# Shared expert at the head of each slot, and the second half's routing moved into the slots, in a two-layer attention and mixture-of-experts kernel

## The reference, cut to what matters

```
xn = layernorm(x)
x  = x + attention(xn) + ffn(xn)

attention: q, k, v = linear(xn); for each row position the 8 batches attend to
           each other in 16 heads of 8 features; then an output product and bias
ffn:       scores  = sigmoid(xn @ w_gate.T)                  # 16 experts
           allowed = the 2 of 4 groups with the highest sum of their two best scores
           chosen  = the 4 best allowed experts; w = their scores / (their sum + 1e-6)
           routed  = sum over experts of w[e] * (silu(xn @ w1[e].T) * (xn @ w3[e].T)) @ w2[e].T
           shared  = (silu(xn @ w1s.T) * (xn @ w3s.T)) @ w2s.T        # no weight
           ffn     = routed + shared
```

## Time and profile before

| what | value |
|---|---|
| median of 3 executions | 382.11 us (381.07 to 382.5) |
| the profiled execution's own time | 381.5 us |
| its span, first to last instruction | 379.7 us |
| mean granted TensorE clock | 0.968 |
| stage one, until the last chunk's `xT_lo` is done | about 170 us |
| stage two, from PE's first gate product to the last DVE instruction | 174.2 to 377.0 us |
| busy in the span: DVE, PE, POOL, ACT | 317.0, 311.3, 244.4, 188.2 us |

### The profile page before, as it was taken

The page is one execution under the profiler, slowest core; times in us unless marked ns, Lnnn a source line. Parts: engine busy times, 40 slices in busy tenths (PEclk is TensorE's granted clock), DMA queues, the critical chain, the costliest instruction groups (busy, mean ns, idle before and its releaser), DMA issues.

```text
span 379.7 us, 5029 instructions
## 1 busy us (share of the span) xinstructions
PE 311.3 (82%) x1435; PEld 226.0 (60%) x1435; DVE 317.0 (83%) x831; ACT 188.2 (50%) x505; POOL 244.4 (64%) x162
## 2 busy tenths in 40 slices
PE   0177777798988987776598898899999999899894
PEld 0045665696776966665365565575766666576562
DVE  3874899969787576974899999989898998989792
ACT  0553756768687668546153253352635253352621
POOL 9144758737356371005388876889998898987661
PEclk9996999999999999869699999999999999999999
DMA  7740000000000000001871331543535343334001
GB/s 189 239 136 0 1 2 1 3 1 0 3 0 3 0 2 1 0 2 54 166 182 56 94 89 58 137 102 97 105 81 135 92 106 90 96 102 135 1 24 31
DMA packets 20367, 24.81 MB, mean 65 GB/s; under 512 B 2140, under 2 KB 11028, under 8 KB 20340
## 3 DMA queue, kind: packets, MB, share of 16 engines
q1 hardware_dynamic: 18544, 23.53, 23.9%
q0 software_dynamic: 544, 0.43, 0.7%
q10 hardware_dynamic: 1252, 0.53, 0.5%
HBM read 22.13 MB, written 2.36 MB: 64 GB/s over the span
## 4 chain that ended last, share of the span: by engine, by line
DVE 35%; PE 35%; issue 11%; ACT 9%; POOL 4%; DMA 3%; ACTq 1%; SPq 1%; DVEq 0%; POOLq 0%
PE Q L871 15%; PE VK L871 7%; PE T L871 5%; DVE att L1495 4%; PE ND L871 4%; DVE hid L1532 4%; DVE sgc L1519 3%; POOL prod_qk L811 3%; DVE rope_a L1274 3%; DVE rope_b L1276 3%; PE T L867 2%; DVE attn L1306 1%; DMA headmask<-in_c_headsel 1%; ACT L707 1%; ACT xn L565 1%
## 5 line engine op out<-in xcount | busy, mean ns | idle before, releaser
L811 POOL TENSOR_TENSOR prod_qk<-qkv 128x1024 f32<-128x1024 f32 x32 | 76.2, 2396 | 21.1 <-ACT qkv L526 12.2
L821 POOL TENSOR_TENSOR prod_pv<-prob,qkv 128x1024 f32<-128x1024 f32 x32 | 69.6, 2195 | 16.5 <-DVE att L1495 15.0
L871 PE MATMUL VK<-hid,w 128*128 128x512 f32 x144 | 74.6, 599 | 0.9 <-DVE hid L1532 0.9
L707 ACT ACTIVATE ND<-Q 128x512 f32<-128x512 f32 x64 | 37.2, 582 | 74.8 <-PE Q L871 58.7
L871 PE MATMUL Q<-xT_hi,w_hi 128*128 128x512 f32 x72 | 52.1, 723 | 1.2 <-issue 0.7
L1519 DVE TENSOR_TENSOR sgc<-ND,cw 128x512 f32<-128x512 f32 x64 | 43.6, 681 | 6.5 <-ACT ND L707 5.0
L1532 DVE TENSOR_TENSOR hid<-T,sgc 128x512 f32<-128x512 f32 x64 | 43.4, 678 | 0.3 <-issue 0.2
L871 PE MATMUL Q<-bias,ones 128*128 128x400 f32 (+1 forms) x64 | 29.9, 467 | 16.7 <-DVE xT_lo L1325 9.1
L1481 DVE TENSOR_REDUCE scr<-prod_qk 128x128 f32<-128x1024 f32 x32 | 38.8, 1212 | 4.5 <-POOL prod_qk L811 4.4
L871 PE MATMUL T<-xT_hi,w_hi 128*128 128x512 f32 x72 | 30.5, 423 | 13.0 <-DVE hid L1532 13.0
L1495 DVE TENSOR_REDUCE att<-prod_pv 128x128 f32<-128x1024 f32 x32 | 38.2, 1195 | 0.0
(11 more groups left out here) (184 smaller groups left out, 755.2 us busy)
## 6 DMA issues: line engine op xcount, KB each, us to landing
cw<-comb_table SPq DMA_DIRECT2D x64, 256.0 KB, 4.6
out_x<-fin SPq DMA_DIRECT2D x8, 256.0 KB, 4.4
x<-in_x SPq DMA_DIRECT2D x2, 256.0 KB, 4.6
wraw<-in_w1T SPq DMA_DIRECT2D x1, 512.0 KB, 10.3
w3raw<-in_w3T SPq DMA_DIRECT2D x1, 512.0 KB, 5.7
w<-in_w2T SPq DMA_DIRECT2D x1, 512.0 KB, 6.4
rope_c<-in_c_cos SPq DMA_DIRECT2D x1, 256.0 KB, 5.0
rope_s<-in_c_sin ACTq DMA_DIRECT2D x1, 256.0 KB, 5.6
```

The costliest lines, as they stand in the source:

```text
L707: act.activation(gated[:, :], QB[side(n, s)][:, :], ACT.Silu).then_inc(sg_ready, 1)
L811: pool.tensor_tensor(prod_qk[:, t % 2], bc(qkv2[:, TH * half + t, j, 0:D], 1, NB), qkv2[:, :, j, D:2 * D], ALU.mult).then_inc(qk_prod, 1)
L821: pool.tensor_tensor(prod_pv[:, t % 2].rearrange("p (h e) b -> p b h e", e=HD), bc(prob[:, t].rearrange("p h b -> p b h"), 3, HD), qkv2[:, ...
L871: return pe.matmul(o, lhsT, rhs, start=start, stop=stop)
```

## The change

Four edits. The shared slice becomes s = 0 and the routed ones s = 1 to 8, so the first slice of stage two needs no weights from the table. The transposes of the first half's weights, and ACT's evacuation of them, move ahead of the last chunk's four `l1_tile`s. PE starts stage two when all but the last of these tiles are evacuated, and waits for the last before slice 1. On ACT, `sigmoid(1)` moves from ahead of the loop to slice 6, behind that slice's Silu and ahead of the first exponential; on DVE the second half's routing, whose first three parts stood ahead of the loop and whose others stood at slices 0 to 16, moves to slices 8 to 22; the second transposes of weights move from slice 20 to 28 (`COMB_AT`), and PE's first wait for them from unit 1 to unit 2.

```diff
-        COMB_AT = BASE[0] + 15
+        COMB_AT = BASE[1] + 14
+        def routed_slice(s):
+            return s - 1
...
-                l1_tile(0)(NB - 1)
-                l1_tile(1)(NB - 1)
                 combT_evac(0)
-                l1_tile(2)(NB - 1)
-                l1_tile(3)(NB - 1)
+                for j in range(NJ):
+                    l1_tile(j)(NB - 1)
...
-            sigmoid(1)
             exp_done = exp_of(act)
             def gate(n, s):
                 act.wait_ge(g_ps, NS * n + s + 1)
-                if s >= 2:
-                    act.wait_ge(sgc_ready, (NS - 1) * n + s - 1)
+                if s >= 3:
+                    act.wait_ge(sgc_ready, (NS - 1) * n + s - 2)
                 else:
                     after(act, hid_ready, NS * n + s - 1)
-                gated = SB[side(n, s)] if s < NS - 1 else sg
+                gated = SB[side(n, s)] if s > 0 else sg
...
                     if p == 1:
+                        if u == 0:
+                            sigmoid(1)
                         exp_done(u)
...
+                if at(i, STEPS - 1):
+                    comb_transposes(0)
                 run(i, 4, l1_tile(0))
                 run(i, 2, output_product)
                 run(i, 4, l1_tile(1))
-                if at(i, STEPS - 1):
-                    comb_transposes(0)
...
-            pe.wait_ge(l1_kept, NT)
+            pe.wait_ge(l1_kept, NT - 1)
...
-                w = slice(s * P, (s + 1) * P)
+                at = routed_slice(s) % NS
+                w = slice(at * P, (at + 1) * P)
+                if n == 0 and s == 1:
+                    pe.wait_ge(l1_kept, NT)
...
-                        if u == 1:
+                        if u == 2:
                             pe.wait_ge(combT_ready, 2)
...
                 if k == COMB_AT:
-                    pe.wait_ge(fin_ready, 1)
+                    pe.wait_ge(fin_ready, 2)
...
             def weighted(n, s, k):
-                if s < NS - 1:
+                if s > 0:
+                    r = routed_slice(s)
                     dve.wait_ge(sg_ready, NS * n + s + 1)
-                    if s % 2 == 0:
-                        dve.wait_ge(ld_cw[s // 2], 32 * (n + 1))
+                    if r % 2 == 0:
+                        dve.wait_ge(ld_cw[r // 2], 32 * (n + 1))
...
             def route_second(k):
-                if k == 0:
+                if k == 8:
+                    route_pairs(1)
+                if k == 9:
+                    route_groups(1)
+                if k == 10:
+                    route_above(1)
+                if k == 11:
                     route_limits(1)
-                if k == 1:
+                if k == 12:
                     route_masked(1)
-                if k == 5:
+                if k == 13:
                     route_top(1)
-                if k in (9, 11):
-                    route_chosen(1, (9, 11).index(k))
-                if k == 13:
+                if k in (15, 17):
+                    route_chosen(1, (15, 17).index(k))
+                if k == 19:
                     route_weights(1)
-                if k == 14:
+                if k == 20:
                     route_sums(1)
-                if k == 15:
+                if k == 21:
                     route_parts(1)
-                if k == 16:
+                if k == 22:
                     route_comb(1)
...
-            route_pairs(1)
-            route_groups(1)
-            route_above(1)
             for k in range(LAST):
```

More of the change, by code:

```diff
@@ L1044, in down @@
                     after(pe, yT_ready, n)
-                mm(VK[:, :], w2[:, s, :], hid[:, s % 3, :], s == 0, s == NS - 1).then_inc(y_ps, 1)
+                mm(VK[:, :], w2[:, routed_slice(s) % NS, :], hid[:, s % 3, :], s == 0, s == NS - 1).then_inc(y_ps, 1)
             def down_two_before(n, s):
@@ L1513, in weighted @@
             def weighted(n, s, k):
-                if s < NS - 1:
+                if s > 0:
+                    r = routed_slice(s)
                     dve.wait_ge(sg_ready, NS * n + s + 1)
-                    if s % 2 == 0:
-                        dve.wait_ge(ld_cw[s // 2], 32 * (n + 1))
-                    V.tensor_tensor(sgc[:, k, :], SB[k][:, :], cw[:, s // 2, s % 2, :], ALU.mult)\
+                    if r % 2 == 0:
+                        dve.wait_ge(ld_cw[r // 2], 32 * (n + 1))
+                    V.tensor_tensor(sgc[:, k, :], SB[k][:, :], cw[:, r // 2, r % 2, :], ALU.mult)\
                         .then_inc(sgc_ready, 1)
             def hidden(n, s, k):
-                if s < NS - 1:
-                    dve.wait_ge(sgc_ready, (NS - 1) * n + s + 1)
+                if s > 0:
+                    dve.wait_ge(sgc_ready, (NS - 1) * n + s)
                 else:
@@ L1530, in hidden @@
                 after(dve, y_ps, NS * n + s - 2)
-                src = sgc[:, k, :] if s < NS - 1 else sg[:, :]
+                src = sgc[:, k, :] if s > 0 else sg[:, :]
                 V.tensor_tensor(hid[:, s % 3, :], UB[k][:, :], src, ALU.mult)\
```

## The result

The changed kernel takes 387.58 us (median of 4 executions, 386.19 to 387.97), the kernel before 381.59 (4, 380.64 to 382.5) beside it: ratio 1.0135, interval 1.0109 to 1.0161. It is slower by 1.35%, 6.0 us. The profiled execution took 387.23, its span is 385.4.

The account below looks back on a forecast made before the run. DVE was taken to set the pace while the second half's routing runs. -4.2 + 4.5 - 0.3 + 0.6 + 3.4 = +4.0 us gave 385.5 from the profiled 381.5, or 386.1 on the median's scale; range 381.0 to 390.0.

Parts of the forecast that it names:

- Steps 1 and 2: Start of stage two: weights leave 2.68 us earlier, first `sgc` at 179.5; shared slice's `hid` (0.60) done in DVE's wait.
- Steps 3 and 4: Slices 1 to 7: DVE ready at 192.95, but Sigmoid in ACT's list puts `sgc` 7 at 195.6: -4.2 us.
- Step 5: Second half's routing in slices 8 to 22 costs DVE +4.5 us at unblocked lengths; filled idle time gives -0.3.
- The `sgc` that DVE owes: By `sgc` 7 DVE has done one `sgc` fewer than before; it shows in the last slice: +0.6 us.
- Step 6: Routing instructions blocked by POOL's products: pairs +2.1, above +1.2, limits and masked +0.1, together +3.4 us (0 to 7.2).
- counted as unchanged: Routing parts in slices 19 to 22, weights to `comb`, were partly blocked before too: no change in cost.
- rival B: Later slots close up with the shared slice first, at most 1.0 us per slot, six over six slots; chance 0.16.
- A: Rival: the moved routing isn't blocked by POOL, so the sum is +0.6 and the time 382.7 us; chance 0.27.
- C: Rival: exponential needs no table load behind Sigmoid; `sgc` 7 comes 1.3 us earlier, 384.8; within the forecast's 0.57.
- The edits at nothing: Later second weight transposes and the gate's wait for `hid` cost nothing; the two trips end by slice 33, needed at 37.

Follow-up runs that it names:

- the kernel with the group scores in PSUM: Changed kernel with the second half's group scores reduced a second time into a PSUM bank, which above reads as one input; 384.84 us, ratio 1.0065.
- POOL held twice: Changed kernel with POOL's third value product of unit 0 held until pairs are done and its next score product until above is done; 383.07 us, ratio 1.0027.
- POOL held once: Changed kernel with POOL's next score product in unit 0 held until above is done; 387.54 us, ratio 1.013.
- the version that beats both: Changed kernel with sigmoid and routing, also limits and masked, ahead of the loop, and POOL's second score product held until masked is done; 378.12 us, ratio 0.9889.
- the first weights early alone: Kernel before, with only the first weights' transposes and their evacuation moved ahead of the last four tiles; 380.44 us, ratio 0.9957.
- late again: Changed kernel with the first weights' transposes and their evacuation put back between the last tiles; 392.21 us, ratio 1.0268.
- the version with the shared slice last: The version that beats both, but with the shared slice last in each slot again; 378.22 us, ratio 0.9894.

## Why the prediction was right, step by step

The sign and the forecast were right, and no rival came true. The sum was +4.0, and the two traces differ by 5.7; the terms are compared with the trace of after. Their errors cancel in part: two are 0.4 too high, two came out 1.85 and 0.75 too low.

**Steps 1 and 2 held.** The transposes stand at 168.94, the first `sgc` starts at 179.40 (179.5), the shared slice's `hid` ends at 176.76 (176.5).

**Steps 3 and 4 held.** `sgc` 7 starts at 195.25 with 2.37 of wait for ACT in front (195.6 and 2.65): -4.6 for -4.2. From Silu 6 to `sgc` 7 it takes 6.19, for 6.15. PE didn't come back slowly: its first up pass took 0.49 after 2.54 of waiting. That it didn't was luck in part: with the same code, in the kernel with the group scores in PSUM, it did after 2.41, and `sgc` 7 came 0.8 later. (For that case the prediction added 1.65, where its rows give 4.06 - 2.25 = 1.81; the range hardly changes by it.)

**Step 5** was 0.4 too high. Counted from the start of each piece to the start of what follows it, and unblocked, the routing takes 4.1 in the slots and not 4.5: pairs 0.64 and above 0.63 (with POOL held twice), groups 0.46, limits 0.57 (1.27 less the 0.7 below), masked 0.33, top 1.44. The first half's rows hold pauses between the pieces that the slots don't have. With the blocked terms below it adds up: 4.1 - 0.3 + 6.65 - 1.4 = 9.05 from `sgc` 7 to `sgc` 23, and the windows give 53.04 - 44.03 = 9.01. The `sgc` that DVE owes, 0.6, stands.

**Step 6 is the one that was mis-sized.** Pairs: 2.21 less the 0.26 of the third one alone, +1.95 for +2.1; it was the third instruction that was caught, not the second. Above: +1.2 was taken from bounds of 0 and 4.4, nearer to 0, "because no row shows instructions this small beside POOL". From the first of above to `hid` it is 212.07 - 207.42 = 4.65, and 206.41 - 205.78 = 0.63 with POOL held: **+4.0**. Size is no cover: an instruction of 16 elements waited for a whole product. And the reason was wrong as it stood, for the trace of before has such a row:

```profile
223.21 0.95 DVE L1416 TENSOR_SCALAR wsum<-wsum 128x16 f32<-128x16 f32 x1
```

It took 0.18 in the first half and ends here at 224.16, with a POOL product that ran from 221.76 to 224.14. Here the rule of the Trainium skill (SBUF — State Buffer, SBUF: two separate sides) was the better guide, and the sentence that gave its term, nearer to 4.4, has the right number; the kernel with the group scores in PSUM agrees with its condition too, since one input outside SBUF was enough to pass at 0.17 to 0.20. Limits: 0.92 less 0.20, +0.7 for +0.1.

**What "counted as unchanged" gave back.** Weights to `comb` met POOL less often than before: `comb` 0.41 for 1.43, and the other two 0.38 less in sum: -1.4.

So step 6 was +6.65 - 1.4 = +5.25 in place of +3.4. The last piece, +0.75, is what the shared slice first costs at slices 44 and 53: the version with it first and the one with it last show it with no routing in it. It was named, as what speaks against rival B, and wasn't in the sum. -4.6 + 9.0 + 0.6 + 0.75 = +5.75; the last `fin` is 5.73 later.

**The rivals.** A needed short instructions beside a busy POOL: the trace shows blocked ones, and taking most of the blocking away gives 383.07, close to A's 382.7. The closeness is luck: in that kernel the limit is still blocked for 2 us, and without that the terms as measured give about -0.85 (-4.6 + 4.1 - 0.3 - 1.4 + 0.6 + 0.75) where A had +0.6. B needed later slots below 22.8; they take 23.8 and 23.3 as before. C needed the exponential to do without a load: there is one at 191.40. The trace agrees with the Trainium skill (ScalarE: Activation LUTs, Table sets: the hidden batching unit) in that Sigmoid and Exp have different sets.

**The edits at nothing.** DVE's idle time in front of `sgc` that ended with `cw` is 2.64 in sum, all at the first: no later transfer was late. The groups of the page of after show it:

```profile
L1526 DVE TENSOR_TENSOR sgc<-ND,cw 128x512 f32<-128x512 f32 x64 | 43.5, 680 | 9.7 <-ACT ND L708 7.0
```

9.7 of idle time, 7.0 of it ended by ACT.

**Where the gain went.** The first weights were really early, worth 1.5 alone. But DVE's wait for them had been the place for the routing, free of charge; moved into slices that DVE paces, its pieces cost their full length, and met POOL besides.

**What stays open.** Why three of four executions with POOL held once showed none of the 2.4 us that the fourth gained. And why PE's clock falls after a wait in one execution and not in another.

## What to carry to other kernels

Before work is moved out of a wait, look for what the engine does in its new place: an idle stretch that looks like a stall may be where work is done for nothing. An instruction's price is the one it has beside its neighbours there: a small VectorE instruction with both inputs in SBUF can cost as much as the GpSimd instruction that runs beside it, so hold GpSimd for the microsecond that the small ones need, or put one input in PSUM. And when one start comes earlier, move into the shorter wait what still fits: here pairs to masked, 3.8 us, and the time fell by 1.1%.

## What the runs showed of the hardware

- Of DVE's small instructions beside a busy POOL, `TENSOR_TENSOR` with both inputs in SBUF waited (0.18 became 2.37), with one in PSUM it didn't (0.17). The limit, a `TENSOR_SCALAR` with one SBUF input, was blocked as well: 0.92, 2.25 and 2.26 where it takes 0.20 alone. A `TENSOR_REDUCE` wasn't: rank took 0.40 and 0.41 beside the products in the two kernels with POOL held, and 0.42 in the first half, alone.
- POOL gets in between two DVE instructions that follow each other without idle time: at 209.36 its second product and the second of above were both due, and POOL went first.
- PE's wait alone doesn't tell whether its clock falls. It kept 2.4 GHz after waits of 1.65 us (the version that beats both) and 2.54 (the changed kernel), and came back at 1.2 GHz after 4.19 (the first weights early alone) and 4.91 (late again), for 5.4 and 5.8 us. Between these it went either way: after 2.41 in the kernel with the group scores in PSUM and 2.51 in the version with the shared slice last, the granted clock was 0.73 over the 6 us that follow. Nor does what PE did just in front of the wait. The two traces of the changed kernel have the same wait, 2.08 us up to 198.31 and 198.49, with PE busy for 6.07 and 6.05 of the 6.20 us in front; over the next 6 us the granted clock was 1.00 in the first and 0.75 in the second.
